# Slot attention inside a four-part transformer kernel: three looped steps become one straight program, worked batch by batch

## The reference, cut to what matters

```python
scale = D ** (-0.5)
x_in = _ln(ctx, lnkv_g, lnkv_b)              # 77 rows a batch
k = x_in @ wk + bk;  v = x_in @ wv + bv
slots = q_mu + jnp.exp(q_logsig) * layernorm(x)      # 512 rows a batch
for _ in range(3):
    prev = slots
    q = _ln(slots, lnq_g, lnq_b) @ wq + bq
    attn = softmax(k @ q / scale over the slots) + EPS_ATTN
    attn = attn / attn.sum(over the context)
    slots = (attn @ v) @ wu + bu + prev
    h = _ln(slots, lnm_g, lnm_b) @ w1 + b1
    slots = gelu(h) @ w2 + b2 + slots
    slots = _ln(slots + cond, lnp_g, lnp_b)
```

## Time and profile before

| what | us |
|---|---|
| median of 3 runs (2538.14 to 2542.62) | 2539.81 |
| the profiled execution, its own time | 2541.59 |
| its span, first to last instruction | 2539.9 |
| PE busy (share of the span) | 2029.3 (80%) |
| DVE busy | 1752.8 (69%) |
| ACT busy | 1524.3 (60%) |
| POOL busy | 826.9 (33%) |

### The profile page before, as it was taken

The page is one execution under the profiler, slowest core; times in us unless marked ns, Lnnn a source line. Parts: engine busy times, 40 slices in busy tenths (PEclk is TensorE's granted clock), DMA queues, the critical chain, the costliest instruction groups (busy, mean ns, idle before and its releaser), DMA issues. The chain is left out here.

```text
span 2539.9 us, 38556 instructions
## 1 busy us (share of the span) xinstructions
PE 2029.3 (80%) x14042; PEld 898.0 (35%) x14042; DVE 1752.8 (69%) x3368; ACT 1524.3 (60%) x1907; POOL 826.9 (33%) x1232
## 2 busy tenths in 40 slices
PE   2344499953879999999999999999999999986312
PEld 1223276731223333333333333333333343332101
DVE  6777411134678888888878887888878887742498
ACT  1122133311558888788777888788788877774133
POOL 4011000012134445443434444344434444322143
PEclk9666699976799999999999999999999999996655
DMA  1000101002243334333343335333433234311000
GB/s 46 1 0 0 34 1 33 0 28 62 40 91 84 78 86 81 82 79 77 82 86 70 65 85 104 85 75 73 86 86 85 66 73 81 74 27 26 24 0 17
DMA packets 147917, 144.34 MB, mean 57 GB/s; under 512 B 30807, under 2 KB 135699, under 8 KB 147731
## 3 DMA queue, kind: packets, MB, share of 16 engines
q1 hardware_dynamic: 147743, 142.05, 25.1%
HBM read 79.01 MB, written 60.51 MB: 55 GB/s over the span
## 5 line engine op out<-in xcount | busy, mean ns | idle before, releaser
L1295 ACT ACTIVATE big<-ps 128x1024 f32<-128x1024 f32 x960 | 955.6, 1027 | 259.3 <-PE ps L1080 238.8
L1481 DVE TENSOR_REDUCE smax<-ps 128x2 f32<-128x1024 f32 x768 | 921.8, 1221 | 270.8 <-PE ps L1069 265.2
L1116 PE MATMUL ps<-big,vaug 128*32 128x512 f32 x3072 | 413.7, 617 | 3.2 <-ACT big L1295 3.1
L1069 PE MATMUL ps<-k,q 49*128 49x512 bf16 x1536 | 294.5, 391 | 64.1 <-DVE smax L1481 34.5
L1080 PE MATMUL ps<-q,k 52*128 52x512 bf16 x1536 | 295.6, 388 | 9.9 <-DVE smax L1481 4.7
L1440 POOL CAST mparts<-smax 128x16 bf16<-128x16 f32 x96 | 19.0, 198 | 577.9 <-DVE smax L1481 577.9
L1069 PEld LDWEIGHTS ps<-k,q 49*128 49x128 bf16 x1536 | 72.7, 94 | 312.0 <-DVE smax L1481 106.6
L625 DVE SCALAR_TENSOR_TENSOR state<-ps,share,state 128x128 f32<-128x128 f32 x128 | 36.0, 344 | 202.6 <-PE ps L596 202.6
L1488 DVE TENSOR_REDUCE maxima<-ps 128x8 f32<-128x616 f32 x192 | 144.8, 795 | 36.9 <-PE ps L1103 35.3
L1194 PE MATMUL ps<-xnT,w 128*128 128x512 f32 x288 | 165.9, 662 | 1.7 <-ACT xnT L1332 1.7
L613 ACT ACTIVATE big<-ps 128x512 f32<-128x512 f32 x128 | 76.5, 598 | 145.1 <-PE ps L587 145.1
(11 more groups left out here) (265 smaller groups left out, 3020.7 us busy)
## 6 DMA issues: line engine op xcount, KB each, us to landing
q<-scratch_queries SPq DMA_DIRECT2D x48, 384.0 KB, 6.1
k<-scratch_keys SPq DMA_DIRECT2D x48, 384.0 KB
cq<-scratch_cross_queries SPq DMA_DIRECT2D x48, 384.0 KB, 5.9
scratch_queries<-rparts SPq DMA_DIRECT2D x24, 384.0 KB, 2.4
scratch_keys<-rparts SPq DMA_DIRECT2D x24, 384.0 KB, 2.5
scratch_cross_queries<-rparts SPq DMA_DIRECT2D x24, 384.0 KB, 2.5
scratch_queries<-rparts SPq DMA_DIRECT2D x24, 256.0 KB, 2.7
scratch_keys<-rparts SPq DMA_DIRECT2D x24, 256.0 KB, 3.0
```

The costliest lines, as they stand in the source:

```text
L1069: last = nc.tensor.matmul(out[:, u], m.q6[rows, v % 2, 2 * g + pr, qt * P:(qt + 1) * P], m.k6[rows, v % 2, 2 * g + pr, :], start=True, sto ...
L1116: last = nc.tensor.matmul(m.ps[32 * j:32 * j + 32, pv_bank, :], of_head(m.vaug, v % 2 * TB + kt, g, j), of_quad("self", q)[:, j, :], start ...
L1295: nc.scalar.activation(of_quad(kind, p // 2)[:, p % 2 * 2:p % 2 * 2 + 2, :], banks("exp" if kind == "self" else "cross exp", p), ACT.Exp, ...
L1481: nc.vector.tensor_reduce(m.smax[:, n % 2, qt, :, pr], banks("max", i), AX.X, ALU.max).then_inc(s_read["self"], 1)
```

## The change

1. The three steps are one straight program (`slot_steps`) in one stage, with no loop, no block end between attention and feed-forward, and no barrier between steps. Semaphores count on over all steps.
2. Every batch passes through all stages on its own: statistics, root, `hat` and the rest are done for the 4 tiles of a batch, and each batch has two PSUM banks to itself (`2 * b` and `2 * b + 1`).
3. The root goes from DVE to POOL (`add`, then `pow` by -0.5, on 128 x 4). For the feed-forward's statistics POOL also makes the shift, -mean times root (two more instructions).
4. The feed-forward's `hat` goes from DVE to ACT (`activation` Identity with shift and root from SBUF, one a tile).
5. The last gain and bias go from DVE (two of 128 x 2048) to POOL (two of 128 x 512 a batch).
6. POOL's two additions to the state are gone. `bu` is added to the values once, in the preparation, by DVE in place of ACT's copy. `cond_rows` comes into the second product as a matmul of one contracted row (`ones32` by `cond_rows`) ahead of the four, accumulated in PSUM.

```diff
-            act.wait_ge(vu_ps, 1)
-            nc.scalar.copy(m.slot_v[0:N_CTX, :, 0:D], m.ps[0:N_CTX, 4, :].rearrange("n (b d) -> n b d", b=B)).then_inc(kv_sb, 1)
...
+            dve.memset(m.ones32[:], 1.0)
...
+            dve.wait_ge(vu_ps, 1)
+            dve.tensor_tensor(m.slot_v[0:N_CTX, :, 0:D], m.ps[0:N_CTX, 4, :].rearrange("n (b d) -> n b d", b=B),
+                              m.rows0[0:N_CTX, 4:5, :].to_broadcast([N_CTX, B, D]), ALU.add).then_inc(kv_sb, 1)
...
+            def down(s, b):
+                pe.wait_ge(h_sb, count(s, b))
+                nc.tensor.matmul(m.ps[:, 2 * b, :], m.ones32[0:1, :], m.cond_rows[0:1, b:b + 1, :].to_broadcast([1, TB, D]),
+                                 start=True, stop=False)
+                for t in range(TB):
+                    last = nc.tensor.matmul(m.ps[:, 2 * b, t * P:(t + 1) * P], m.qT[:, b, t * P:(t + 1) * P], m.mats0[:, 5, :],
+                                            start=False, stop=(t == TB - 1))
+                last.then_inc(out_ps, 1)
...
+            def normal(s, b):
+                act.wait_ge(root_m, count(s, b))
+                for t in range(b * TB, (b + 1) * TB):
+                    last = nc.scalar.activation(m.hat[:, t, :], m.state[:, t, :], ACT.Identity, bias=m.shift[:, t:t + 1],
+                                                scale=m.st.rstd[:, t:t + 1])
+                last.then_inc(hat_m, 1)
...
+            def root(s, b, moments, ready):
+                pool.wait_ge(moments, count(s, b))
+                chain.link(add_epsilon(b))
+                power(b).then_inc(ready, 1)
+
+            def root_and_shift(s, b):
+                pool.wait_ge(moments_m, count(s, b))
+                nc.gpsimd.tensor_scalar(tiles(m.shift, b), tiles(m.st.mv, b)[:, :, 0], -1.0, None, ALU.mult)
+                chain.link(add_epsilon(b))
+                chain.link(power(b))
+                nc.gpsimd.tensor_tensor(tiles(m.shift, b), tiles(m.shift, b), tiles(m.st.rstd, b), ALU.mult).then_inc(root_m, 1)
+
+            def last_gain(s, b):
+                pool.wait_ge(hat_p, count(s, b))
+                hat = tiles(m.hat, b)
+                chain.link(nc.gpsimd.tensor_tensor(hat, hat, m.rows0[:, 2:3, :].to_broadcast([P, TB, D]), ALU.mult))
+                nc.gpsimd.tensor_tensor(tiles(m.state, b), hat, m.rows0[:, 3:4, :].to_broadcast([P, TB, D]), ALU.add).then_inc(gained, 1)
...
+                for b in range(B):
+                    root_and_shift(s, b)
+                for k in range(B + 2):
+                    if k < B:
+                        root(s, k, moments_p, root_p)
+                    if again and 2 <= k - 1:
+                        root(s + 1, k - 3, moments_q, root_q)
+                    if 1 <= k <= B:
+                        last_gain(s, k - 1)
+                if again:
+                    root(s + 1, B - 1, moments_q, root_q)
...
+            for s in range(SLOT_STEPS):
+                again = s + 1 < SLOT_STEPS
+                for k in range(B + 1):
+                    if k < B:
+                        maximum(s, k)
+                    if k >= 1:
+                        divide(s, k - 1)
+                for b in range(B):
+                    add_update(s, b)
+                for k in range(B + 1):
+                    if k < B:
+                        add_output(s, k)
+                    if again and k >= 3:
+                        query_moments(s + 1, k - 3)
+                    if k >= 1:
+                        normal(s, k - 1, root_p, hat_p)
+                if again:
+                    query_moments(s + 1, 2)
+                    normal(s + 1, 0, root_q, hat_q)
+                    query_moments(s + 1, 3)
+                    for b in range(1, B):
+                        normal(s + 1, b, root_q, hat_q)
...
-        with nc.Fori(0, SLOT_STEPS), stage(nc) as sem:
-            slot_step(nc, a, m, sem)
+        with stage(nc) as sem:
+            slot_steps(nc, a, m, sem)
```

More of the change, by code:

```diff
@@ L295, in _ @@
         @block.gpsimd
         def _(pool):
[L298 to L330, removed]
-            for b in range(B):
[L332 to L341, removed]
@@ L343, in _ @@
[L343 to L358 removed]
+            chain = Chain(pool, pch)
@@ new lines, in add_update @@
+            def add_update(s, b):
+                dve.wait_ge(upd, count(s, b))
+                for i in range(2):
+                    both = m.ps[:, 2 * b + 1 - i, :].rearrange("p (t c) -> p t c", t=2)
+                    t = b * TB + 2 * i
+                    last = nc.vector.reciprocal(m.colsum[:, t:t + 2], both[:, :, D])
+                chain.link(last)
+                for t in range(TB):
+                    at = b * TB + t
+                    both = m.ps[:, 2 * b + 1 - t // 2, :].rearrange("p (t c) -> p t c", t=2)
+                    last = nc.vector.scalar_tensor_tensor(out=m.state[:, at, :], in0=both[:, t % 2, 0:D], scalar=m.colsum[:, at:at + 1],
+                                                          in1=m.state[:, at, :], op0=ALU.mult, op1=ALU.add)
+                chain.link(last)
+                moments(b).then_inc(moments_m, 1)
@@ L425, in _, with add_output @@
+            def add_output(s, b):
+                dve.wait_ge(out_ps, count(s, b))
+                chain.link(nc.vector.tensor_tensor(tiles(m.state, b), tiles(m.state, b),
+                                                   m.ps[:, 2 * b, :].rearrange("p (t d) -> p t d", t=TB), ALU.add))
+                moments(b).then_inc(moments_p, 1)
             for k in range(B + 1):
                 if k < B:
-                    act.wait_ge(turned, k + 1)
-                    nc.scalar.activation(m.xnT[:, k, :], m.ps[:, k % 2, :], ACT.Identity, bias=m.cols0[:, 5:6],
-                                         scale=m.cols0[:, 4:5]).then_inc(hin, 1)
@@ L430, in _ @@
-                b = k - 1
-                if b >= 0:
-                    act.wait_ge(h_ps, b + 1)
-                    nc.scalar.activation(m.qT[:, b, :], m.ps[:, 2 + b % 2, :], ACT.Gelu, bias=m.cols0[:, 9:10]).then_inc(h_sb, 1)
-        @block.gpsimd
-        def _(pool):
-            pool.wait_ge(hat, B)
-            for b in range(B):
-                last = nc.gpsimd.tensor_tensor(m.state[:, b * TB:(b + 1) * TB, :], m.state[:, b * TB:(b + 1) * TB, :],
-                                               m.cond_rows[:, b:b + 1, :].to_broadcast([P, TB, D]), ALU.add)
-            last.then_inc(added, 1)
```

202 lines of the change are left out of this document (113 added, 89 removed).

## The result

The changed kernel took 2501.61 us (median of 4 runs, 2493.11 to 2504.66) against 2539.09 (4 runs) of the kernel before on the same chip: a ratio of 0.984, 95% interval 0.982 to 0.986. The profiled execution took 2493.11, with a span of 2491.4.

The account below looks back on a forecast made before the run. The slot steps were taken as bound by a chain hopping between engines, mostly on DVE. Their parts summed to 198.8 us against 210.7; with 0.8 of preparation that is -11.1, hence 2529 us, range 2506 to 2548.

Parts of the forecast that it names:

- lead-in: From the first statistics to the first maximum of the slot steps: to stay at 15.2 us.
- A: From a step's first maximum to the end of the feed-forward's statistics: 19.3 us, then 20.4 twice, against 22.2.
- B: From the end of the feed-forward's statistics to its first addition: 6.6 us a step, against 11.8.
- C: From the feed-forward's first addition to the next step's first `hat`: 25.7 us, against 27.7.
- D: From the next step's first `hat` to its first maximum: 13.5 us, longer than the 8.3 before.
- last end with the stage's end: Last step from the feed-forward's first addition: 24.4 us against 19.6, plus 0.9 for the stage's end.
- The shared port: At DVE's `hat`: every POOL instruction starting between two tiles holds the next tile; some 12 us of waits a step.
- rival 2: At DVE's `hat`: only POOL's long passes hold the port, the `pow` does not; about 2514 us, chance 0.1.
- rival 1: `hat` on DVE does not wait for POOL: slot steps 179.7 us, kernel 2510, chance 0.2.
- I assume the same mixture: PE's clock over the slot steps: grant stays near 0.69, about two fifths of the time at the higher level.
- Rival 3: PE stays at the lower clock in the slot steps: 243.8 us there, kernel 2574, chance 0.11.
- Rival 4: The program fails its purpose, for instance straight code or semaphores costing what the barriers did: 2544 us, chance 0.04.

Follow-up runs that it names:

- Experiment 1: Changed kernel plus a stage timing 16 DVE tiles beside POOL work: `hat` took 4.19 us alone or beside `pow`, 8.1 beside four 512-column multiplications.
- experiment 2: Changed kernel with the last gain and bias back on DVE instead of POOL: slot steps 170.34 us, kernel 2496.46 us.
- the second comparison: Changed kernel run again unaltered, four times, on one chip with the filler kernels: slot steps 171.08 us, whole 2497.17 us, ratio to before 0.984.
- experiments 4: Changed kernel with every root back on DVE, still batch by batch: slot steps 241.99 us, kernel 2564.51 us against 2542.23 before the change.
- experiment 7: Changed kernel with last `hat` on ACT, gain and bias on DVE, next step's first `hat` ahead of the last statistics: slot steps 166.06, kernel 2500.08 us.
- experiment 5: Changed kernel with the feed-forward's `hat` back on DVE in place of ACT: slot steps 196.78 us, kernel 2525.26 us.
- experiment 8: Changed kernel rerun, and three versions with useless PE products in idle time; the one with feed-forward `hat` on DVE: slot steps 176.36, whole 2510.18 us.
- its version with fillers: The kernel of experiment 7 with useless identity products put into PE's idle time: slot steps 162.92 us, whole 2488.79 us, ratio to before 0.981.

## Why the prediction was wrong

The direction, the order of the work and most prices held; the size did not, and the time came in below even the low end of the range. Part by part, the forecast's terms beside the first profile:

| part | forecast | measured | difference |
|---|---|---|---|
| lead-in | 15.2 | 12.0 | -3.2 |
| A, three | 60.1 | 56.2 | -3.9 |
| B, three | 19.8 | 18.6 | -1.2 |
| C, two | 51.4 | 40.1 | -11.3 |
| D, two | 27.0 | 22.3 | -4.7 |
| last end with the stage's end | 25.3 | 21.5 | -3.8 |
| sum | 198.8 | 170.7 | -28.1 |

**The step that failed is "The shared port"**: "I let each whole POOL instruction that starts between two tiles of `hat` hold the next tile." It was carried over from rows in which POOL's passes had 2048 columns to a `pow` on 128 x 4. In C it gave 8.4 a step, and 0.87 + 0.95 = 1.8 were measured (1.95 and 2.03 less 1.08). In D it gave 4.0, and the 3.11 less 1.08 is 2.0. In the last end it gave 7.9, and 3.9 were measured; in the lead-in it took back 2.4, and no tile was held. Term by term that is 23.5 of the 28.1. Experiment 1 shows the mechanism alone, experiment 2 in the program: without the wide passes no tile waits, with all 36 roots in place.

This is rival 2, to which 0.1 was given. Its argument ("reads and writes four numbers a partition") is borne out by experiment 1, and what spoke against it, that DVE had waited for the very end of POOL's instructions, came from wide passes only. The trace had no narrow POOL instruction beside a `tensor_scalar`, so both ends had to stay open; I put 0.55 on one of them.

Rival 2 had the mechanism, but not the number. With its parts (C 21.6, D 13, end 22.4, and lead-in and B as in rival 1) its steps add to about 184.8, and its time was 2514, where 170.7 and 2501.6 were measured. Even rival 1's 179.7, in which no tile waits at all, is 9.0 too long. In these sums other waits of DVE come forward when the port's go, so the rule on the port is worth 14 of the 28.1 there, and not 23.5; how those waits were worked out is not said. The rest is A (3.9), D (3.7), C (3.1, with 4.5 of waits measured where 6.4 were left), the end (1.8), and lead-in and B (0.8 each).

**A** was too long by 1.3 a step. Its own terms do not add up (9.3 and 10.5 are 19.8, and 19.3 was entered). Maxima and divisions end 8.3 after the first maximum (113.03 to 121.3), not 9.3 as before: a batch's division now stands behind the next batch's maximum, so DVE no longer waits 0.84 for the exponential of each batch but only for PE's logits (1.29 and 1.04) and once for the last exponential (0.25); and "about 0.7 in steps two and three" for the exponential's table load was wrong, A being 18.6, 18.9 and 18.7. The four times 2.6 of update and statistics is right to 0.1.

**B** and the prices behind it held: 2.0 for root and shift on POOL, 0.41 a tile on ACT, the table load on the chain. **C** less the port was 1 too short a step: DVE waits 1.29 for POOL's bias, ahead of the third batch's statistics, which the forecast did not have. **D** grew, as forecast, from 8.3 to 10.5 and 11.8.

**"I assume the same mixture"** of the clock was wrong on the good side, 0.76 for 0.69; what that is worth in the changed kernel was not taken apart. Rival 3, the lower level, did not come, but it was near: moving one instruction kind back to DVE brought it, with 20 of the 26 us, and ten idle products took it away again. Its sum of 243.8 can't be redone from the parts that it names: they leave some 17 to 18 us for a lead-in that is not priced.

**Rival 4** fails: the barriers that are gone are worth 4.3, with the overlap over them, and the straight code at most 1.3.

**Behind the steps** the code is the same, and the profiled execution was 9 us shorter there. From the first addition to `x` to the second, and from there to the end, thirteen profiles took 277.0 to 282.6 and 1997.0 to 2004.2, with no tie to what was changed: the kernel before has 279.8 and 2004.2, its written-out loop 281.9 and 2003.9, the changed kernel 277.1 and 1998.0, the version with roots on DVE 277.0 and 1998.1, the one with a stage for each step 282.5 and 2004.2. So one execution's total says little below 10 us here. The medians (-37.5 and, in the second comparison, 2497.17 against 2536.16, -39.0) agree with the steps alone: -40.0 and +0.5. Why the same instructions wander was not followed up.

So the account of the 40 us is this: three roots a step and, in exchange for waits of equal size, gain and bias leave DVE; statistics, root and `hat` of one batch run beside another batch's products; and the barriers go. How the 40 us divide between the first two is not shown. The 71 and 26 us of experiments 4 and 5 do not add up with the rest, since each removes a condition of the others, and the other half of the first test, roots on POOL for all 16 tiles at once, was not run. An estimate: `pow` took 1.04 on 128 x 4 and 5.50 on 128 x 32 (experiment 1), so on a line between them some 3.0 on 128 x 16, more than the 2.5 of DVE's whole root. By that, the move without the batches would gain nothing either.

## What to carry to other kernels

A chain of small dependent instructions costs the same for a quarter of the data, so cut a stage into batches only if that chain leaves the engine that carries the path. A port wait seen in a trace has two shapes, the waiting and the holding one: carry over its price only to instructions of the same kind and width, and where the trace has none, time the pair by itself. And where PE gets its work in pieces, look at its level piece by piece: one engine's four tiles more can cost twice their own time through it.

## What the runs showed of the hardware that was not expected

- POOL's `pow` does not hold DVE's `tensor_scalar`, not even at 5.50 us on 128 x 32, nor do its multiplications and additions on 128 x 4 (4.22 and 4.19 for 16 tiles, 4.19 alone). Its multiplications of 512 columns do (8.1), and its copies of 256 columns hardly do (about 0.3 of 1.48).
- DVE's pass of 512 columns with two SBUF inputs stretches POOL's shortest instructions from 0.23 to 0.65 (experiment 7).
- PE can be busy for 20 us without a gap in the trace and stay at the lower of its levels (5.00 of 5.00 at 0.50, experiment 5, all three steps), while most of the same instructions, with ten products more in the idle time ahead of them, run at the higher (1.12 and 1.16 for 2.07 and 2.08). It can also fall in the middle of such a stretch (experiment 8, 2.08 at 91.85). So the work of a stretch alone does not tell its level.
- The level at the same place differs between executions: the lead-in of experiment 7 and of its version with fillers is the same program up to the first feed-forward, and its first maximum came at 58.44 and 57.14, the two ends of what eleven profiles of that stretch show.
